# One branch of TensorE moved from behind the last layers to the middle of them, in a graph attention kernel

## The chip, the cores and the metric

The kernel runs on one core of a Trainium2 chip, in one launch. The metric is the device time in microseconds, median of three runs. A core has five engines with their own instruction streams: TensorE (matmuls), VectorE, ScalarE, POOL (GpSimd) and SyncE, which here issues the DMAs. They meet only at semaphores. Each engine has a sequencer that works through the stream (waits, branches, register reads) and hands the rest to the engine proper.

## The reference

Two blocks on 2048 nodes with 512 features: `x = x + smooth(relu(layernorm(x)), adj)` and `x = x + attend(relu(layernorm(x)), adj)`. The second one matters here:

```python
Wh = einsum('nf,hfd->hnd', x, W)                       # 8 heads of 64
e = leaky_relu(e_src[:, :, None] + e_dst[:, None, :], 0.2)
att = softmax(where(adj[None] > 0, e, -9e15), axis=-1)
h = elu(einsum('hnm,hmd->hnd', att, Wh))
enc = transpose(h, (1, 0, 2)).reshape(2048, 512)
out = relu(enc @ W1.T + b1)     # 512 -> 256
out = relu(out @ W2.T + b2)     # 256 -> 128
out = relu(out @ W3.T + b3)     # 128 -> 256
out = out @ W4.T + b4           # 256 -> 512
```

## The kernel before, in words

The attention is computed in factored form without a row maximum, which holds while the exponents and the row sums stay in a safe range. The kernel checks that range. A flag `retry` is 0 when all is in range; when it is 1, an exact attention (`attend_exactly`, a loop over tiles and heads) and the dense layers are computed again and the output is stored again. With the inputs given the flag is 0 and that path is jumped over.

After the attention the four dense layers run on four chunks of 512 nodes each, c = 0 to 3 (`CHUNKS` is 4). Class `Dense` holds the steps: `turn` transposes a quarter of the chunk's encoding, `sum1(c, m)` is one half of the first layer (12 matmuls), `sum2(c)` the second layer (6), `sum3(c)` the third (6), `sum_row(c, t)` the fourth layer for one tile of 128 nodes (6, and twice 6 half-wide ones for the last tile). Each product is split in high and low parts, hence three matmuls where one would stand. ScalarE applies the ReLUs (lines 2350 to 2367), VectorE cuts the low parts (2372 to 2382) and adds the residual rows (`finish_row`, 2290), POOL adds the bias to the residual (2297) and cuts two low parts (2301, 2304), SyncE stores the rows (2210), the last two chunks tile by tile, loads the residual (2202) and waits for the last stores (2222). The order on each engine is written out by hand; TensorE's stands in `dense_layers`, which takes the chunks interleaved: the next chunk's first layer between this chunk's second and third.

The flag is made like this. VectorE counts the row sums in range, per partition, into `fine_sum`; ahead of the third chunk's second layer (c = 2) TensorE adds the partitions up with a matmul of one column (line 1985); VectorE compares the count with what it should be and writes `retry` (line 1513). It raises `retry_chain`, on which the engines wait before they ask for the flag. To ask for it an engine reads the flag into a register and branches, in the helper `if_set`, line 86. VectorE does so at once, and has its remaining layer work in both arms of the branch. TensorE waits on `retry_chain` ahead of `sum3(2)`, since that writes the bank in which the count stood, but asks for the flag only behind all its layers, at line 2029. ScalarE, POOL and SyncE ask behind their last work too. The block's end (line 1327) is a drain on each engine and a meeting of all.

Of the kernel before, what the change touches and what calls it, by code (L numbers as in the profile page):

```python
# [81 lines left out]
def if_set(eng, flag):  # L82

    if flag is None:
        return nullcontext()
    return eng.If(eng.value_load(flag[0:1, 0:1], min_val=0, max_val=1) > 0)
# [1043 lines left out]
def attend_and_finish(nc, before, bank, wh, e, mask, ident, adj, e_rows, fac, wh_store, x1_store, weights, weight_parts, small, out):  # L1130
# [10 lines left out]
    with ExitStack() as ctx:  # L1141
# [3 lines left out]
        def sem(name):  # L1145
            return ctx.enter_context(nc.semaphore(name))
# [26 lines left out]
        retry, fine_sum, safe = small  # L1173
# [12 lines left out]
        with ExitStack() as later:  # L1186
            exact = attend_exactly(nc, ctx, later, bank, wh, e, ident, adj, e_rows, wh_store)
        exact_sync, exact_vector, exact_scalar, exact_tensor, exact_done = exact
        (parts_odd,), (_, e_late, _, *first_early), (res_odd, o3_hi, o3_lo, o2_hi, o2_lo, _) = one_place(
            nc, ctx, [("l4_parts1", [P, T, 2 * PW], F32R)],  # L1190
            [("l4_to_e_late", [P, 4224], F32), ("l4_e_late", [2 * H, 2 * QW], F32), ("l4_to_first", [P, 1024], F32), ("l4_first_a", [P, T - QUAD, HE], F32), ("l4_first_c", [P, T - QUAD, HE], F32)],
# [5 lines left out]
        src = sb("l4_src", [P, 2, QW])  # L1197
        o_m = sb("l4_o_m", [P, GT, PW])
        (whole,), (last_neg, _) = one_place(
            nc, ctx, [("l4_whole", [P, T, HE], F32)],  # L1200
            [("l5_last_neg", [P, 2, H, HD], F32), ("l5_rest_whole", [P, T], F32)])
# [54 lines left out]
        retry_chain = sem("l5_retry_chain")  # L1256
        fine_counted = sem("l5_fine_counted")
        dense_buffers = (share, neg, last_neg, (hi_even, hi_odd), (lo_even, lo_odd), (o1_hi, o1_lo), (o2_hi, o2_lo), (o3_hi, o3_lo), whole_o, (res_even, res_odd),
                         w1_hi, w1_lo, (w2_hi, w2_lo), (w3_hi, w3_lo), (w4_hi, w4_lo), b1_s, b2_s, b3_s, b4_s)
        dense = Dense(nc, ctx, "l5", EARLY, bank, wh, ident, dense_buffers)  # L1260
        again = Dense(nc, ctx, "l7", 0, bank, wh, ident, dense_buffers)
        CHUNKS = dense.NCH
# [64 lines left out]
        with nc.Block() as block:  # L1327
# [531 lines left out]
            def _(pe):  # L1859
# [109 lines left out]
                            pe.wait_ge(m_bank_free, GT * (LAST + 2))  # L1969
                        dense.turn(pe, 0, i // 2 - 2)  # L1970

                def dense_layers(of):
                    of.sum1(pe, 0, 0)
                    of.turn(pe, 1, 0)
                    of.turn(pe, 1, 1)
                    of.sum1(pe, 0, 1)
                    of.turn(pe, 1, 2)
                    of.turn(pe, 1, 3)
                    if of is dense:
                        pe.wait_ge(q_bank_free, GT * (2 * LAST + 3))  # L1980
                        pe.wait_ge(w_lo_ready, 4)
                    for c in range(CHUNKS - 1):
                        if of is dense and c == CHUNKS - 2:
                            pe.wait_ge(retry_chain, CHUNKS + 1)
                            pe.matmul(bank[of.SUM3_BANKS[0]][0:1, 0:1], fine_sum[:], safe[:], start=True, stop=True
                                      ).then_inc(fine_counted, 1)
                        of.sum2(pe, c)
                        of.sum1(pe, c + 1, 0)
                        if of is dense and c == CHUNKS - 2:
                            pe.wait_ge(retry_chain, CHUNKS + 2)  # L1990
                        of.sum3(pe, c)
                        of.sum1(pe, c + 1, 1)
                        of.sum_row(pe, c, 0)
                        if c + 2 < CHUNKS:
                            of.turn(pe, c + 2, 0)
                            of.turn(pe, c + 2, 1)
                        else:
                            of.sum2(pe, c + 1)
                        of.sum_row(pe, c, 1)
                        if c + 2 < CHUNKS:  # L2000
                            of.turn(pe, c + 2, 2)
                            of.turn(pe, c + 2, 3)
                        of.sum_row(pe, c, 2)
                        if c + 2 == CHUNKS:
                            of.sum3(pe, c + 1)
                        of.sum_row(pe, c, 3)
                    for t in range(GT):
                        of.sum_row(pe, CHUNKS - 1, t)

                pe.wait_ge(first_lo, 2)  # L2010
                for r in range(2):
# [12 lines left out]

                pe.wait_ge(w_loaded, 16 * 8)
                pe.wait_ge(w_lo_ready, 1)
                dense_layers(dense)
                pe.wait_ge(retry_chain, CHUNKS + 2)
                with if_set(pe, retry):
                    exact_tensor(pe)  # L2030
                    for k in range(KC):
                        again.turn(pe, 0, k)
                    dense_layers(again)


def attend_exactly(nc, ctx, tiles, bank, wh, e, ident, adj, e_rows, wh_store):
# [490 lines left out]
```

## Time and profile before

| | us |
|---|---|
| median of 3 runs | 861.61 (861.1 to 862.35) |
| the profiled execution | 862.1 |
| its span | 860.3 |
| TensorE busy | 839.7 |
| VectorE busy | 700.0 |
| ScalarE busy | 428.7 |
| POOL busy | 281.0 |

The profile is of one execution, whose own time is 862.1 us; the span, from the first to the last instruction of the program, is 1.8 us shorter. Times inside the trace count from the span's start. PE is TensorE's matmul, PEld its weight load, which overlaps the matmul before it; a q behind an engine's name is its sequencer. Register reads, branches, waits and DMA issues are not counted as busy; the view by source line shows them nevertheless. q1 are the data's DMA queues, q8 and q14 those by which instructions are fetched.

### The profile page before, as it was taken

Reading aid. Unit: us, or ns where it says so; the run is one execution under the profiler, and the core shown is the slowest. Engines: PE = TensorE matmul, PEld = TensorE weight load, DVE = VectorE, ACT = ScalarE, POOL = GpSimd, SP = SyncE. Lnnn points to the kernel's source line nnn. Section 1 sums busy time; section 2 is a strip of 40 time slices with the busy share of each in tenths; the row PEclk is TensorE's granted clock in tenths of the full one; section 3 lists DMA queues with packets and bytes.
Section 4 is the critical chain, followed back from the end, with each engine's and each line's share of the span. In section 5 each row is a group of like instructions: output and inputs, shape, how many; then the busy total and the mean of one; then the engine's idle time right before and its main releaser. Section 6 shows DMA issues by size and latency. Waiting matters only on the chain.

```text
span 860.3 us, 15286 instructions
## 1 busy us (share of the span) xinstructions
PE 839.7 (98%) x5208; PEld 756.5 (88%) x5208; DVE 700.0 (81%) x1222; ACT 428.7 (50%) x797; POOL 281.0 (33%) x299
## 2 busy tenths in 40 slices
PE   2999999999999999999999999999999999999997
PEld 2888888888888888888899999999999999999786
DVE  6899886557656886586999999999999999998864
ACT  3445433221111112257766666666666666775753
POOL 0000000000000000057875555555556654566422
PEclk9999999999999999999999999999999999999999
DMA  8979931703222222053310000000000032000134
GB/s 344 406 272 375 362 98 50 219 0 122 96 97 92 95 93 89 0 196 126 129 27 25 23 16 26 26 24 25 26 26 25 24 93 68 26 2 6 45 148 149
DMA packets 37675, 87.97 MB, mean 102 GB/s; under 512 B 7216, under 2 KB 8368, under 8 KB 37616
## 3 DMA queue, kind: packets, MB, share of 16 engines
q1 hardware_dynamic: 37616, 87.24, 28.5%
q8 instruction: 30, 0.49, 0.2%
q14 instruction: 29, 0.24, 0.1%
HBM read 74.45 MB, written 12.78 MB: 101 GB/s over the span
## 4 chain that ended last, share of the span: by engine, by line
PE 97%; DMA 1%; DVE 1%; ACT 1%; SPq 0%; issue 0%
PE bank L1877 29%; PE bank L1921 14%; PE bank L77 13%; PE bank L79 13%; PE bank L78 13%; PE bank L554 3%; PE bank L1082 2%; PE bank L1087 2%; PE bank L1083 2%; DMA l_kept<-adj 1%; PE bank L1033 1%; PE bank L2455 1%; PE bank L2449 1%; PE bank L2394 1%; PE bank L2451 1%; PE bank L2420 0%
## 5 line engine op out<-in xcount | busy, mean ns | idle before, releaser
L1397 DVE SCALAR_TENSOR_TENSOR l_q<-bank,e,mask 128x512 fp32r<-128x512 f32 x512 | 339.0, 740 | 22.9 <-PE bank L1877 22.9
L1877 PE MATMUL bank<-l_parts,l_q 128*128 128x260 f32 x2048 | 249.6, 283 | 0.0
L1877 PEld LDWEIGHTS bank<-l_parts,l_q 128*128 128x128 f32 x2048 | 246.7, 188 | 0.4
L77 PE MATMUL bank<-x_hi,s_hi 128*128 128x512 f32 x448 | 174.4, 389 | 0.0
L79 PE MATMUL bank<-x_hi,s_lo 128*128 128x512 f32 x448 | 174.3, 389 | 0.0
L78 PE MATMUL bank<-x_lo,s_hi 128*128 128x512 f32 x448 | 174.3, 389 | 0.0
L805 POOL TENSOR_TENSOR l_prod<-wh,l_a 128x512 f32<-128x512 f32 x29 | 34.0, 1195 | 379.5 <-ACT wh L757 379.5
L1565 ACT ACTIVATE l_o_q<-bank 128x260 f32<-128x260 f32 x128 | 49.0, 388 | 104.0 <-PE bank L1877 96.7
L79 PEld LDWEIGHTS bank<-x_hi,s_lo 128*128 128x128 f32 x448 | 84.1, 188 | 17.6
L78 PEld LDWEIGHTS bank<-x_lo,s_hi 128*128 128x128 f32 x448 | 84.1, 188 | 17.3
L77 PEld LDWEIGHTS bank<-x_hi,s_hi 128*128 128x128 f32 x448 | 84.1, 188 | 17.3
L734 ACT ACTIVATE s_hi<-rows 128x1024 fp32r<-128x1024 f32 x28 | 29.7, 1062 | 122.5 <-PE bank L79 122.5
L1559 ACT ACTIVATE l_mask_near<-mask 128x512 fp32r (+1 forms) x128 | 70.1, 621 | 1.3 <-DVE l_nmr L878 0.9
L1559 ACT ACTIVATE l_mask_far<-mask 128x512 fp32r (+1 forms) x128 | 69.9, 619 | 0.0
L1921 PE MATMUL bank<-l_parts,l_mask_far 128*128 128x260 f32 x512 | 67.7, 284 | 0.0
L1921 PE MATMUL bank<-l_parts,l_mask_near 128*128 128x260 f32 x512 | 67.3, 283 | 0.0
L1921 PEld LDWEIGHTS bank<-l_parts,l_mask_far 128*128 128x128 f32 x512 | 64.6, 189 | 0.0
L1921 PEld LDWEIGHTS bank<-l_parts,l_mask_near 128*128 128x128 f32 x512 | 64.3, 188 | 0.0
L824 DVE CAST x_hi<-G 128x512 fp32r<-128x512 f32 (+1 forms) x32 | 13.6, 426 | 50.8 <-PE bank L79 48.2
L1311 POOL TENSOR_TENSOR l_o_m<-l_o_m 128x520 f32<-128x520 f32 x16 | 18.5, 1157 | 82.3 <-ACT l_o_m L1572 82.3
L829 DVE TENSOR_TENSOR s_lo<-rows,s_hi 128x1024 fp32r<-128x1024 f32 x32 | 39.1, 1223 | 0.2 <-ACT s_hi L734 0.2
L463 ACT ACTIVATE s_hi<-l_now 128x1024 fp32r<-128x1024 f32 x16 | 17.0, 1060 | 39.1 <-PE bank L79 32.1
(234 smaller groups left out, 1179.8 us busy)
## 6 DMA issues: line engine op xcount, KB each, us to landing
rows<-adj_t SPq DMA_DIRECT2D x48, 512.0 KB, 3.8
l_now<-adj SPq DMA_DIRECT2D x16, 512.0 KB, 7.5
l_rows_k<-adj_t SPq DMA_DIRECT2D x16, 512.0 KB, 8.3
l_src<-e_rows SPq DMA_DIRECT2D x32, 256.0 KB, 3.2
l_kept<-adj SPq DMA_DIRECT2D x12, 512.0 KB, 13.2
wh_store<-wh SPq DMA_DIRECT2D x4, 1040.0 KB, 6.2
l_h<-x SPq DMA_DIRECT2D x4, 1024.0 KB, 17.3
x<-x SPq DMA_DIRECT2D x1, 4096.0 KB, 13.7
```

Of the source, the lines that this page charges most:

```text
L77: pe.matmul(acc, hi, rhs_hi, start=first, stop=False, skip_group_check=True)
L78: pe.matmul(acc, hi, rhs_lo, start=False, stop=False, skip_group_check=True)
L79: return pe.matmul(acc, lo, rhs_hi, start=False, stop=True, skip_group_check=True)
L554: mm = pe.matmul(bank[k][:], left[:, b, k * P:(k + 1) * P], right[:, s, :], start=s == 0 and n == 0, stop=n == 2, skip_group_check=True)
L734: a.activation(a_hi[:, r % 2, :], rows[:, r, :], ACT.Copy).then_inc(hi_ready, 1)
L805: p.tensor_tensor(per_head(prod[:, b, n, :]), wh[:, t, :, 0:HD], per_head(a_b[:, n, :]), ALU.mult).then_inc(prod_ready, 1)
L829: v.tensor_tensor(a_lo[:, b, :], rows[:, r, :], a_hi[:, b, :].bitcast(F32), ALU.subtract).then_inc(lo_ready, 1)
L1397: v.scalar_tensor_tensor(out=q[:, i, :], in0=bank[S_BANKS[hh]][:], scalar=e[:, i, H + h:H + h + 1], in1=mask[:, i, cols], op0=ALU.is_le, o ...
L1559: a.activation(mask_slot(i), mask[:, i, cols], ACT.Copy).then_inc(m_ready, 1)
L1565: a.activation(o_q[hh][:, t, :], bank[Q_BANKS[hh][t]][:, 0:PW], ACT.Copy).then_inc(q_bank_free, 1)
L1877: return pe.matmul(bank[Q_BANKS[hh][t]][:, 0:PW], q[:, i, t * P:(t + 1) * P], parts[pair_slot][:, i, hh * PW:(hh + 1) * PW], start=i == 0, ...
L1921: return pe.matmul(bank[M_BANKS[t]][:, 0:PW], mask_slot(i)[:, t * P:(t + 1) * P], parts[pair_slot][:, i, BOTH_C], start=i == 0, stop=i == ...
```

## The change

`dense_layers` is cut in two. `layers_up_to_count` holds everything up to the third chunk's second layer and the first half of the fourth chunk's first layer, with the matmul that counts ahead of them; `layers_from_count` holds the rest, from the third chunk's third layer on. TensorE now waits on `retry_chain` and asks for the flag between the two. The second part stands in both arms: with the flag set the exact path follows it, with the flag clear it is the `Else` arm. The order of the matmuls is the same as before in either case, and no other engine's program is changed.

```diff
-                def dense_layers(of):
+                def layers_up_to_count(of):
...
-                    for c in range(CHUNKS - 1):
-                        if of is dense and c == CHUNKS - 2:
-                            pe.wait_ge(retry_chain, CHUNKS + 1)
-                            pe.matmul(bank[of.SUM3_BANKS[0]][0:1, 0:1], fine_sum[:], safe[:], start=True, stop=True
-                                      ).then_inc(fine_counted, 1)
+                    for c in range(CHUNKS - 2):
                         of.sum2(pe, c)
                         of.sum1(pe, c + 1, 0)
-                        if of is dense and c == CHUNKS - 2:
-                            pe.wait_ge(retry_chain, CHUNKS + 2)
                         of.sum3(pe, c)
...
+                    if of is dense:
+                        pe.wait_ge(retry_chain, CHUNKS + 1)
+                        pe.matmul(bank[of.SUM3_BANKS[0]][0:1, 0:1], fine_sum[:], safe[:], start=True, stop=True
+                                  ).then_inc(fine_counted, 1)
+                    of.sum2(pe, CHUNKS - 2)
+                    of.sum1(pe, CHUNKS - 1, 0)
+
+                def layers_from_count(of):
+                    c = CHUNKS - 2
+                    of.sum3(pe, c)
+                    of.sum1(pe, c + 1, 1)
+                    of.sum_row(pe, c, 0)
+                    of.sum2(pe, c + 1)
+                    of.sum_row(pe, c, 1)
+                    of.sum_row(pe, c, 2)
+                    of.sum3(pe, c + 1)
+                    of.sum_row(pe, c, 3)
                     for t in range(GT):
-                        of.sum_row(pe, CHUNKS - 1, t)
+                        of.sum_row(pe, c + 1, t)
...
-                dense_layers(dense)
+                layers_up_to_count(dense)
                 pe.wait_ge(retry_chain, CHUNKS + 2)
                 with if_set(pe, retry):
+                    layers_from_count(dense)
                     exact_tensor(pe)
                     for k in range(KC):
                         again.turn(pe, 0, k)
-                    dense_layers(again)
+                    layers_up_to_count(again)
+                    layers_from_count(again)
+                with pe.Else():
+                    layers_from_count(dense)
```

## Rows read from the trace of the kernel before

**Rows 1.** The page: busy time, share, instructions; the chain's shares by engine.
```profile
PE 839.7 (98%) x5208; PEld 756.5 (88%) x5208; DVE 700.0 (81%) x1222; ACT 428.7 (50%) x797; POOL 281.0 (33%) x299
...
PE 97%; DMA 1%; DVE 1%; ACT 1%; SPq 0%; issue 0%
```
**Rows 2.** Line 86: operation, count: ns min/median/max, first and last start in us.
```profile
L86 DVEq TENSOR_LOAD <-retry x1: 550/550/550, 834.0 to 834.0; - x1
...
L86 DVEq COMPARE_BRANCH  x1: 56/56/56, 834.9 to 834.9; - x1
...
L86 PEldq TENSOR_LOAD <-retry x1: 482/482/482, 854.1 to 854.1; - x1
...
L86 PEldq COMPARE_BRANCH  x1: 4147/4147/4147, 855.0 to 855.0; - x1
```
**Rows 3.** Line 1327, the end of the block.
```profile
L1327 PEldq DRAIN  x1: 72/72/72, 859.2 to 859.2; - x1
...
L1327 SPq DRAIN  x1: 7/7/7, 860.1 to 860.1; - x1
```
**Rows 4.** DMA queues in the window 856.0 to 856.1: packets, MB, share of 16 engines.
```profile
q8 instruction: 1, 0.02, 107.6%
```
**Rows 5.** Timeline 832.5 to 833.9: start us, length us, engine, line, operation, tiles.
```profile
833.80 0.14 DVE L1513 TENSOR_SCALAR retry<-bank 1x1 int32<-1x1 f32 x1
```
**Rows 6.** Line 2236 in the window 832 to 834, TensorE's sequencer.
```profile
L2236 PEldq EVENT_SEMAPHORE  x1: 2393/2393/2393, 833.2 to 833.2; - x1
```
**Rows 7.** Timeline: the third layer's first weight load; the last two matmuls.
```profile
837.14 0.19 PEld L2431 LDWEIGHTS bank<-l_o_hi,l_w_hi 128*128 128x128 f32 x1
...
855.35 0.40 PE L2455 MATMUL bank<-l_w_hi,l_o_lo 128*128 128x256 f32 x2
```
**Rows 8.** Timeline of SyncE at 833.91; DMA queues in 835.0 to 837.8.
```profile
833.91 0.38 SPq L2210 DMA_DIRECT2D out<-l_res  x1
...
q1 hardware_dynamic: 496, 0.99, 94.6%
```
**Rows 9.** DMA queues in 837.8 to 838.2; timeline of VectorE with its idle time.
```profile
q14 instruction: 1, 0.01, 4.8%
...
839.99 0.69 DVE L2382 TENSOR_TENSOR l_o_lo<-bank,l_o_hi 128x512 fp32r<-128x512 f32 x1 [6.05 <-ACT bank L2367]
```
**Rows 10.** DMA queues in 830 to 831.
```profile
q8 instruction: 1, 0.02, 8.2%
```
**Rows 11.** Timeline of POOL, VectorE and TensorE's weight loads in 844 to 851.
```profile
844.02 4.63 POOL L2297 TENSOR_TENSOR l_res<-l_res,l_b 128x2048 f32<-128x2048 f32 x1 [3.82 <-DMA l_res<-x_store]
...
850.81 1.44 DVE L2290 TENSOR_TENSOR l_res<-bank,l_res 128x512 f32<-128x512 f32 x2
...
850.95 0.19 PEld L2455 LDWEIGHTS bank<-l_w_hi,l_o_lo 128*128 128x128 f32 x1 [0.43 <-DVE l_o_lo L2382]
```
**Rows 12.** Line 2210: all stores; landing of that in 846 to 847; in 856 to 857.
```profile
L2210 SPq DMA_DIRECT2D out<-l_res x11: 332/333/1869, 818.2 to 856.2; - x11
...
DMA to landing us min/median/max: 2.0/2.0/2.0
...
DMA to landing us min/median/max: 3.6/3.6/3.6
```
**Rows 13.** DMA packets in 857.2 to 857.75; line 2222, the wait for the last store.
```profile
DMA packets 1, 0.00 MB, mean 4 GB/s; under 512 B 0, under 2 KB 0, under 8 KB 1
...
L2222 SPq EVENT_SEMAPHORE  x1: 17/17/17, 859.9 to 859.9; - x1
```
**Rows 14.** Engines' busy time by window (matmuls of one tile), then all; PEclk after PE.
```profile
16.00:18.00 2.00, 2.00 (x5) 1.61 (x6) 0.00 (x0) 0.00 (x0) 1.00 1.03 410
18.00:20.00 2.00, 2.00 (x6) 1.52 (x6) 0.00 (x0) 0.00 (x0) 1.00 1.03 410
...
22.00:24.00 2.00, 2.00 (x11) 1.65 (x10) 0.00 (x0) 0.00 (x0) 1.00 1.03 410
...
856.00:860.30 4.30, 0.00 (x0) 0.00 (x0) 0.21 (x1) 0.00 (x0) 0.00 (x0) 1.00 0.36 118
```

More of the change, by code:

```diff
@@ L1993, in dense_layers @@
                         of.sum_row(pe, c, 0)
[L1994 to L1998, printed above, removed]
+                        of.turn(pe, c + 2, 0)
+                        of.turn(pe, c + 2, 1)
                         of.sum_row(pe, c, 1)
-                        if c + 2 < CHUNKS:
-                            of.turn(pe, c + 2, 2)
-                            of.turn(pe, c + 2, 3)
+                        of.turn(pe, c + 2, 2)
+                        of.turn(pe, c + 2, 3)
                         of.sum_row(pe, c, 2)
-                        if c + 2 == CHUNKS:
-                            of.sum3(pe, c + 1)
                         of.sum_row(pe, c, 3)
+                    if of is dense:
[14 more added lines that the diff above has]
+                    of.sum_row(pe, c, 3)
                     for t in range(GT):
-                        of.sum_row(pe, CHUNKS - 1, t)
+                        of.sum_row(pe, c + 1, t)
                 pe.wait_ge(first_lo, 2)
```

## The prediction, made before the result was known

> **What bounds the kernel now.** I read the page first: its busy times and the chain that ended last [rows 1]. TensorE is busy for 98% of the span and holds 97% of the chain, so nearly every microsecond in which TensorE stands in the last layers reaches the end. The timeline of 820 to 861 us says the same of the place of the change: weight load follows weight load every 0.23 us, and the flag is made beside it.
>
> The second view is by source line, since a branch is not counted as busy. Line 86 reads the flag into a register and branches [rows 2]. On VectorE the pair begins at 834.0 and the branch itself is booked with 56 ns. On TensorE it stands at the end of everything: the read begins at 854.1, the branch at 855.0, and the branch is booked with 4147 ns. TensorE's drain follows at 859.2 while SyncE's own drain is at 860.1 [rows 3]. So TensorE's closing branch does not end the kernel itself. It is what the change moves into the middle of the layers.
>
> The third view is the DMA activity in short windows, because such a branch has a visible cause: an instruction fetch. A 16 KB packet on the instruction queue q8 starts in the window 856.0 to 856.1; it takes 107.6% of 16 engines over 0.1 us, which is 1.72 us on one [rows 4]. It starts 1.0 us after the branch, and the branch ends (855.0 + 4.15 = 859.15) 3.1 us after the fetch began.
>
> **The change part by part.**
>
> *Order of the matmuls.* They are the same ones in the same order on the path taken here (flag clear). Two conditionals on the chunk number disappear at build time. Cost 0, with nothing that could hide one: no queue but TensorE's is touched. DMAs, SyncE and POOL keep their programs.
>
> *What stands between flag and branch.* The flag is ready at 833.80 + 0.14 = 833.94 [rows 5], and VectorE's read starts at 834.0. TensorE's sequencer can be there in time, because it runs ahead of its array: an event of the third chunk's third layer (line 2236), which stands behind all of the third chunk's second layer and the first half of the fourth's first, is already under way at 833.2 [rows 6], while the first matmul of that third layer loads its weights only at 837.14 [rows 7]. The end of the kernel agrees: the read at 854.1 comes while the last two matmuls run from 855.35 on. So I start TensorE's new read at 834.0 and its branch 0.9 us later (854.1 to 855.0), at 834.9. Until 837.14 the array has work queued. That is a cover of 2.2 us from the branch on.
>
> *The branch.* With the 4.15 us of rows 2 it would end at 839.05, the next weight load would come about 0.1 later, and TensorE would stand for 839.1 - 837.1 = 2.0 us. But there is a difference in what the DMA engines do. The new branch falls into the 1 MB store issued at 833.91: from 835.0 to 837.8 data packets hold 94.6% of the 16 engines and no code packet is seen [rows 8]. VectorE's branch of 834.9 jumps over a large body as well, and the first code packet of any engine after it starts between 837.8 and 838.2, behind the store [rows 9], 3 us after the branch and not 1.0. VectorE never shows this, since it waited for ScalarE's second relu half until 839.99 anyway [rows 9]. I take that packet to be VectorE's, and let TensorE's fetch wait as long. From its start the branch takes 3.1 us by rows 4, less what a quieter queue saves: a 16 KB fetch in the window 830 to 831 took 8.2% of 16 engines, 1.3 us instead of 1.72 [rows 10]. So 837.8 + 2.8 = 840.6, and TensorE stands for 840.6 - 837.2 = 3.4 us. Bounds: 0 if the branch were as short as VectorE's 56 ns (833.94 + 0.9 + 0.1 = 834.9, all covered); 2.0 with a prompt fetch; 3.9 with 3.1 us from the fetch's start; 5.3 if the array had to be empty before the read (837.5 + 0.9 + 4.15 = 842.5 against 837.2). I take 3.4, nearest to rows 8 and 9.
>
> *Behind the branch.* Queued behind it are TensorE's last 84 matmuls; ScalarE waits for the third layer, VectorE for rest and rows, SyncE for the rows to store. Nothing absorbs: TensorE's waits after 838, such as the 0.43 us at 850.95 [rows 11], are for results of matmuls that themselves move. The bias addition of the last chunk on POOL (844.02, 4.63 long) is due at 850.81 [rows 11], so a residual load delayed by the fetch has 2.2 us of air, and 3.4 more after the shift. The stall goes to the end in full.
>
> *What leaves the end.* The last stores do not land like the others. A store issued in 846 to 847 lands in 2.0 us; the last one, issued at 856.24, takes 3.6, and its issue takes 1869 ns where the median is 333 [rows 12]. This is the time of the 16 KB fetch of TensorE's closing branch. Between 857.2 and 857.75 just one data packet is seen in 0.55 us, when 128 KB or more should be moving [rows 13]: one engine holds back its part and the issue stands behind it. SyncE finds the last landing at 859.9 [rows 13], 0.4 before the end. With the closing branch gone, the store should land in 2.0 to 2.2 us: 3.6 - 2.05 = 1.55 us saved. SyncE's own read and branch, 0.9 us as on the other engines, move up with the issue: 856.6 + 0.9 = 857.5, before the landing at 858.3. Bounds 0 (SyncE's issue was slow for a reason of its own) and 1.6.
>
> *Sum.* 862.1 (the profiled execution: span 860.3 and 1.8 around it) + 3.4 - 1.55 = 863.95. The median of the runs, 861.61, lies 0.5 below the profiled one, which gives 863.45; I say 863.4, 0.21% slower.
>
> The Trainium skill, page "Runtime: NRT & Kernel Launch", section "Instruction fetch mechanics", says a taken branch whose target is outside the current 2-page window forces a DMA fetch, and gives TensorE 128 KiB for instructions. The trace agrees with the fetch (4147 ns). If it were the 128 KiB that counted, the target could be at hand, which is rival B.
>
> **The rivals.**
>
> *A, the fetch is prompt.* It goes ahead of the store's packets as at 856.0, where stores were moving too. The stall is 2.0: 862.1 + 2.0 - 1.55 = 862.55, by the median 862.05, no change. For it: the only measured TensorE case. Against it: the empty code queues of rows 8. It decides at the fetch's start: before 837 it is A, behind it the forecast.
>
> *B, the branch finds its target.* All is covered by the queued matmuls and only the end changes: 861.6 - 1.55 = 860.05, faster by 0.18%, and just over 0.2% if the end gives back 0.2 more. Against it: the same kind of jump missed at 855.0, and the new one spans more. This is the mechanism on the other side; it holds as long as the branch is under 2.2 us.
>
> *C, the end gives nothing back.* The slow issue was SyncE's own, or a prefetch of TensorE's next page falls into the last 2 us: 861.6 + 3.4 = 865.0, or 863.6 with A's stall. For it: SyncE's code may miss as well; against: the single trickling packets just while q8 was fetching.
>
> *D, a second stop.* If the branch's target lies near the end of its page, TensorE runs dry again while the next page comes, by an estimate from the fetch above (1.3 us, and the 1.4 from the fetch's end at 857.7 to the branch's at 859.15) 2 to 3 us: 865.4 to 866.4. At 0.23 us for a weight load with its matmul, that is the last two dozen instructions of a page.
>
> *E, the clock.* TensorE starts at half its later rate, though the clock's column prints 1.00 there: 5 matmuls from 16 to 18 us and 6 from 18 to 20, 11 from 22 to 24 [rows 14]. If it fell from 2.4 to 1.2 GHz after the stop and stayed there for those 4 us, that costs 2 more, 865.4. Against it: after the last matmul the granted clock stays 1.00 over 4.3 idle us [rows 14].
>
> The Trainium skill, "TensorE: Matmul & The Clock Gate", section "Why this matters for your kernels", warns that idle gaps between matmul bursts put the clock back; by it E would be the outcome. The trace shows no stop of that length in mid-kernel, and none at its end that cost clock.
>
> **How the numbers follow.** Forecast 0.40, A 0.27, B 0.08, C 0.10, D 0.10, E 0.05. A measurement of this kernel tells about 0.2% (1.7 us) from no change, so 863.35 is the line. The forecast (862.9 to 864.1 by its bounds) lies on both sides of it: 0.23 slower, 0.17 same. A is same. B gives 0.06 faster, 0.02 same. C splits 0.08 to 0.02; D and E are slower by 0.13, and 0.02 of D is same with A's stall. Together 0.06 faster, 0.50 same, 0.44 slower. The range goes from B's edge to D: 860.6 to 865.6.
>
> **What would show it.** In the changed trace, line 86 on TensorE: its read at 834.0 and a branch of 5.5 to 6.1 us (A: 4.1; B: under 0.3). The q8 packet behind 837.6 (A: before 836.5). An idle time before line 2431's weight load of 3.4 us (A: 2.0). The last store's issue at 0.33 us and its landing at 2.0 to 2.2 us. TensorE's count and order of matmuls unchanged. The forecast fails if TensorE does not stand at the branch, or if the last store still takes 3.6 us to land.

## The result and the profile after

The changed kernel takes 866.56 us (median; 865.96 to 866.91), the kernel before 861.63: a ratio of 1.0056, with a 95% interval of 1.0043 to 1.0069. It is slower by 4.9 us. The forecast was 863.4 with a range to 865.6, so the time lies outside it. The profiled execution took 866.76 us, with a span of 864.8 against 860.3.

The page after: TensorE's busy time grew from 839.7 to 842.7 us with the same number of matmuls [rows 1], which no stop alone can do. VectorE's did not move.

```profile
PE 842.7 (97%) x5208; PEld 758.7 (88%) x5208; DVE 700.0 (81%) x1222; ACT 429.2 (50%) x797; POOL 281.4 (33%) x299
...
PE 97%; DVE 1%; DMA 1%; ACT 1%; issue 1%
```

By line, line 86 after (answers to rows 2) and the drains of line 1327 (rows 3):

```profile
L86 DVEq TENSOR_LOAD <-retry x1: 552/552/552, 833.6 to 833.6; - x1
L86 PEldq TENSOR_LOAD <-retry x1: 478/478/478, 833.6 to 833.6; - x1
...
L86 PEldq COMPARE_BRANCH  x1: 5710/5710/5710, 834.5 to 834.5; - x1
...
L1327 PEldq DRAIN  x1: 1682/1682/1682, 860.0 to 860.0; - x1
```

TensorE reads the flag in the same tenth of a microsecond as VectorE, with matmuls still queued on the array until 837.1, and the branch takes 5.71 us where the closing one took 4.15. Everything up to there lies 0.38 us earlier than in the trace of before. The timeline of TensorE around the stop (start, length, engine, line; in brackets the idle time before):

```profile
836.76 0.39 PE L79 MATMUL bank<-l_enc_t_hi,l_w_lo 128*128 128x512 f32 x1
...
840.30 0.29 PEld L2440 LDWEIGHTS bank<-l_o_hi,l_w_hi 128*128 128x128 f32 x1 [3.58 <-issue]
840.33 0.77 PE L2440 MATMUL bank<-l_o_hi,l_w_hi 128*128 128x512 f32 x1 [3.18 <-issue]
...
840.89 0.63 PE L2441 MATMUL bank<-l_o_hi,l_w_lo 128*128 128x512 f32 x1
...
841.32 0.63 PE L2443 MATMUL bank<-l_o_lo,l_w_hi 128*128 128x512 f32 x1
```

The third layer's first weight load (line 2440, before 2431, rows 7) is at 840.30; without a stop it would be at 837.14 - 0.38 = 836.76. So the stop is 3.5 us. And then the matmuls do not come every 0.23 us but every 0.43. The windows show why (busy time of PE, PEld, DVE, ACT, POOL; then the granted clock, DMA share, GB/s):

```profile
830.00:837.00 7.00, 7.00 (x32) 5.26 (x31) 2.72 (x5) 1.88 (x4) 3.46 (x2) 1.00 0.39 141
837.00:840.30 3.30, 0.14 (x1) 0.00 (x1) 0.00 (x0) 1.27 (x2) 1.34 (x2) 0.90 0.38 60
...
839.50:840.00 0.50, 0.00 (x0) 0.00 (x0) 0.00 (x0) 0.00 (x0) 0.29 (x1) 0.62 0.98 57
...
840.30:846.40 6.10, 6.07 (x14) 4.79 (x15) 1.38 (x2) 2.48 (x4) 2.20 (x1) 0.50 0.42 162
...
850.00:855.00 5.00, 5.00 (x24) 4.14 (x23) 2.14 (x5) 2.53 (x5) 0.00 (x0) 1.00 0.34 132
```

The granted clock was 1.00 (2.4 GHz) until the stop and fell within it: the mean of 0.62 in 839.5 to 840.0 puts the fall at 839.6, 2.5 us after the last matmul's end (836.76 + 0.39 = 837.15). It stood at 0.50 (1.2 GHz) until 846.4, for 6.8 us in all, and in the last 6.1 of them TensorE was working. In these 6.1 us 14 to 15 matmuls ran; at full rate they need 3.4 us.

The q8 packet and the last stores (rows 8, 9, 12 and 13 of before). First the DMA queues: the q1 line is of the window 834.5 to 837.4, which has no q8 or q14 packet, and the q8 and q14 lines are of 837.4 to 838.4. Then line 2219, the stores, with the landing of the last:

```profile
q1 hardware_dynamic: 515, 1.03, 96.0%
...
q8 instruction: 1, 0.02, 5.9%
q14 instruction: 1, 0.01, 1.9%
```
```profile
L2219 SPq DMA_DIRECT2D out<-l_res x11: 332/333/388, 817.9 to 862.2; - x11
...
DMA to landing us min/median/max: 2.2/2.2/2.2
```

No code packet starts while the 1 MB store runs; then one on each code queue does. No store is slow to issue any more, and the last lands in 2.2 us, not 3.6.

No second stop follows: the next q8 packet starts at 843.4, and the weight loads around it keep their distance of 0.43 us.

The balance of the two traces: -0.38 (earlier arrival) + 3.54 (the stop) + 2.76 (the half clock: from the third layer's first weight load to that of the first row it is 847.14 - 840.30 = 6.84 us, before 841.22 - 837.14 = 4.08) - 1.4 (the end: VectorE's last addition at 861.71 against 855.78, 5.93 later, the span's end only 4.5 later) = 4.5 us, the difference of the spans.

### The profile page after: what moved, and what is told of

It reads as the page before. It is cut to its first block, busy times and chain, and to the rows that moved or that the text cites. A ratio compares the mean times of both kernels' runs of the same rounds, so it can differ in the third digit from the quotient of the medians.

```text
span 864.8 us, 15286 instructions
## 1 busy us (share of the span) xinstructions
PE 842.7 (97%) x5208; PEld 758.7 (88%) x5208; DVE 700.0 (81%) x1222; ACT 429.2 (50%) x797; POOL 281.4 (33%) x299
## 4 chain that ended last, share of the span: by engine, by line
PE 97%; DVE 1%; DMA 1%; ACT 1%; issue 1%
PE bank L1877 28%; PE bank L1921 14%; PE bank L79 13%; PE bank L78 13%; PE bank L77 13%; PE bank L554 3%; PE bank L1082 2%; PE bank L1087 2%; PE bank L1083 2%; PE bank L1033 1%; PE bank L2464 1%; PE bank L2458 1%; PE bank L2403 1%; PE bank L2460 1%; DMA l_h<-x 1%
```

## The experiments

Each is compared with the kernel before as timed beside it: its median was 861.39 us for near, no_branch, warm14 and tiles_after, 861.54 for idle, tiles_before and hint, and 861.62 for the other three.

**near: a short jump.** TensorE's arm for a set flag, not taken here, is cut to the layers.

```diff
                     layers_from_count(dense)
-                    exact_tensor(pe)
-                    for k in range(KC):
-                        again.turn(pe, 0, k)
-                    layers_up_to_count(again)
-                    layers_from_count(again)
                 with pe.Else():
```

> The changed kernel, but TensorE's arm for a set flag holds only the layers; the exact path and the repeated layers are left out on TensorE alone (that arm is not taken here). The jump to the clear arm is then short. Theory (the instruction fetch makes the branch long, the stop puts the clock back, and a closing fetch disturbs the last store): TensorE's branch under 0.3 us, no idle time ahead of the third chunk's third layer, granted clock 1.000, last store lands in 2.0 to 2.3 us; 861.6 - 1.45 = 860.2. Rival (a register read and a branch between queued matmuls cost by themselves, wherever the target lies): branch over 4 us or a stop of over 2 us, 864 or more.

860.03 against 861.39 us, ratio 0.9983 (0.9974 to 0.9992), granted clock 1.000. Line 86 and the stores:

```profile
L86 PEldq COMPARE_BRANCH  x1: 461/461/461, 834.7 to 834.7; - x1
```
```profile
L2214 SPq DMA_DIRECT2D out<-l_res x11: 332/332/388, 818.1 to 856.1; - x11
...
DMA to landing us min/median/max: 1.7/1.7/1.7
```

The branch takes 0.46 us (I expected under 0.3), TensorE does not stand at it, and the last store lands in 1.7 us. So a branch at this place costs nothing that shows when its target is near; with the far target it costs the stop and what follows from it.

**no_branch: the end by itself.** The kernel before without TensorE's closing question.

```diff
                 dense_layers(dense)
-                pe.wait_ge(retry_chain, CHUNKS + 2)
-                with if_set(pe, retry):
-                    exact_tensor(pe)
...
-                    dense_layers(again)
```

> The kernel before without TensorE's closing question for the flag (its exact path is left out on TensorE). Theory (the code fetch of TensorE's closing branch holds back one DMA engine, and with it the last store): the last store is issued in 0.33 us and lands in 2.0 to 2.3 us, 861.6 - 1.45 = 860.2. Rival (SyncE's slow issue is its own, and the changed kernel's last store was quicker because it came later): last issue 1.9 us, landing 3.6, 861.6.

860.27, ratio 0.9990 (0.9981 to 0.9999): faster by 0.9 us by the ratio and by 1.1 by the medians, where 1.45 was expected; the interval, 0.1 to 1.6 us, leaves room for both. The longest issue and the last landing:

```profile
L2204 SPq DMA_DIRECT2D out<-l_res x11: 332/332/389, 817.3 to 855.4; - x11
...
DMA to landing us min/median/max: 1.7/1.7/1.7
```

Nothing of SyncE or the stores was touched, and the slow issue (1869 ns) and the slow landing (3.6 us) of rows 12 are gone. So TensorE's closing branch did reach the end of the kernel, through the DMA engine that carried its code.

**warm14: the stop filled.** 14 matmuls whose result is not used are queued ahead of the read.

```diff
                 layers_up_to_count(dense)
+                dense.wait_for_rest(pe, 3, CHUNKS - 3, 1)
+                for n in range(14):
+                    pe.matmul(bank[dense.SUM3_BANKS[1]][:], dense.w1_hi[:, 0, 0:P], dense.enc_t_hi[1][:, 0, :],
+                              start=True, stop=True, skip_group_check=True)
                 pe.wait_ge(retry_chain, CHUNKS + 2)
```

> The changed kernel with 14 matmuls of 512 columns, whose result is not used, queued on TensorE just ahead of the flag's read; they write a bank that the third layer then overwrites. They fill 3.2 us of the 3.5 us stop. Theory (the clock falls because the array stands): branch 5.7 us as before it, third layer begins at 840.3, granted clock 1.000, 866.5 - 2.7 = 863.8; if the queue cannot take them all, the read comes late and it is up to 864.8. Rival (the clock falls for another reason than the idle time, as the fetch or the branch itself): clock 0.996 and 866.5 or more.

864.13, ratio 1.0032 (1.0020 to 1.0044), clock 1.000. With 3.2 us of work more it is 2.4 us faster than the changed kernel. Line 86, then the timeline:

```profile
L86 PEldq TENSOR_LOAD <-retry x1: 864/864/864, 836.7 to 836.7; - x1
...
L86 PEldq COMPARE_BRANCH  x1: 3400/3400/3400, 837.9 to 837.9; - x1
```
```profile
837.56 3.33 PE L2035 MATMUL bank<-l_enc_t_hi,l_w_hi 128*128 128x512 f32 x14
841.48 0.47 PE L2444 MATMUL bank<-l_o_hi,l_w_hi 128*128 128x512 f32 x1 [0.59 <-issue]
841.78 0.40 PE L2445 MATMUL bank<-l_o_hi,l_w_lo 128*128 128x512 f32 x1
```

The flag's read came at 836.7, 2.5 us after VectorE's at 834.2, I take it because the queue could not hold all 14, and the layer begins at 841.5 and not 840.3. What remains is a stop of 0.6 us between matmuls, and behind it they come at full rate. The branch, later than the 1 MB store, takes 3.4 us. It is still a far branch with a code fetch, and the clock holds.

**tiles_after and tiles_before: the store out of the fetch's way.** The second chunk's rows go out in four stores of 256 KB as they are finished.

```diff
-        step = 1 if c >= self.NCH - 2 else self.GT
+        step = 1 if c >= self.NCH - 3 else self.GT
```

with the counts of two waits on the stores' semaphore to match.

> The changed kernel, in which the second chunk's rows are stored tile by tile as they are finished (four stores of 256 KB) and not in one of 1 MB that is issued just before the branch. Theory (the code fetch waits behind the 1 MB store): the fetch starts about 1 us after the branch, the branch takes 4.2 us or little more, TensorE stands 2.0 us; if the clock then holds, 862.3, if it falls all the same 865.0. Rival (the branch takes 5.7 us because of its farther target or the fetch itself): branch 5.7 us, 866.5.

> The kernel before with the second chunk's rows stored tile by tile, the control for the changed kernel with that edit. Theory (that edit matters only where a fetch waits behind the 1 MB store): 861.4, within 0.5. Rival (the four small stores are quicker by themselves and hid a stop): 860 or less.

In the changed kernel: 861.92, ratio 1.0005 (0.9996 to 1.0014), clock 1.000. In the kernel before: 861.91 against 861.54, ratio 1.0004 (0.9995 to 1.0013), no change. Line 86 and the code packets in 835.6 to 836.0, first edit:

```profile
L86 PEldq COMPARE_BRANCH  x1: 3634/3634/3634, 834.6 to 834.6; - x1
```
```profile
q8 instruction: 1, 0.02, 16.6%
q14 instruction: 1, 0.01, 5.9%
```

The third layer's first weight load, and a window behind it:

```profile
838.35 0.19 PEld L2440 LDWEIGHTS bank<-l_o_hi,l_w_hi 128*128 128x128 f32 x1 [1.50 <-issue]
...
838.40:846.00 7.60, 7.60 (x34) 6.30 (x35) 2.67 (x4) 4.34 (x8) 5.93 (x2) 1.00 0.29 109
```

The two code packets start 1.2 us after the branches and not 3.3, TensorE's branch takes 3.6 us and not 5.7, its weight loads stand for 1.5 us (the idle time of line 2440), and the clock holds. The same jump with the same matmuls, and 4.4 to 4.6 us less than the changed kernel (4.4 when each is taken against the kernel before beside it): by the traces 2.0 of the stop and 2.8 of the clock. The control says that the edit has no gain of its own.

**idle: a stop without a branch.** The kernel before with one wait more, ahead of the third chunk's third layer.

```diff
                             pe.wait_ge(retry_chain, CHUNKS + 2)
+                            pe.wait_ge(of.pool_done, of.NCH + 1)
                         of.sum3(pe, c)
```

> The kernel before with one wait more and no branch moved: ahead of the third chunk's third layer TensorE waits for POOL's rest of the fourth chunk's first layer, which ends at 840.2. TensorE then stands about as long as in the changed kernel (weight load at 840.3 and not 837.1), without branch or code fetch there. Theory (any stop of this length puts the clock back): granted clock under 1.000, matmuls every 0.43 us for some us after the stop, 861.4 + 3.1 + 2.7 = 867.2, the last store still landing in 3.6 us. Rival (the clock falls only with the branch or the fetch): clock 1.000, 861.4 + 3.1 = 864.5.

866.35, ratio 1.0046 (1.0033 to 1.0060). The weight loads, and a window behind the stop:

```profile
840.27 0.19 PEld L2432 LDWEIGHTS bank<-l_o_hi,l_w_hi 128*128 128x128 f32 x1 [3.13 <-issue]
...
841.14 0.33 PEld L2432 LDWEIGHTS bank<-l_o_hi,l_w_hi 128*128 128x128 f32 x1
841.57 0.33 PEld L2433 LDWEIGHTS bank<-l_o_hi,l_w_lo 128*128 128x128 f32 x1
```
```profile
840.60:843.80 3.20, 3.20 (x9) 2.43 (x9) 0.69 (x1) 1.95 (x4) 0.00 (x0) 0.50 0.81 314
```

A plain wait puts the clock down as well, here for half as long: finer windows put the fall at 840.5 and the rise at 843.9. That is 3.1 us of stop and some 1.7 of clock (half of 3.4 us), 866.3 with 861.54, and not the 867.2 expected from a clock term of 2.7. And it does not do so every time. Of the five executions four ran at a mean granted clock of 0.998 and took 865.57 to 866.58 us; the fifth kept 1.000 and took 864.35, close to the rival's 864.5. So a stop like this seems able to pass without the loss; that execution has no trace of its own. The closing branch is still there, and so are the last store's slow issue of 1634 ns and slow landing of 3.4 us.

**hint, hint_late, hint_before, hint_before_early: the branch announced.** An instruction ahead of the branch names it as likely taken. In hint it runs at 821.8, 13 us ahead of the branch; in hint_late at 830.6, 4.6 us ahead; in hint_before at 833.1 and in hint_before_early at 817.5, 21 and 38 us ahead of the closing branch. The edit of hint, in the complete changed kernel:

```diff
+                        if of is dense and c == 1:
+                            far_arm.append(pe.mark_branch_hint_location())
                         of.sum1(pe, c + 1, 1)
...
+                asked_in = pe.bass.cur_bb.bb
                 with if_set(pe, retry):
...
+                bass.BassInstruction(asked_in.instructions[-1]).branch_hint(far_arm[0])
```

> The changed kernel, complete, with a branch prefetch hint on TensorE: at the second chunk's third layer, some 10 us ahead of the branch, the branch is announced as likely taken. Theory (only the late fetch of the clear arm costs): if the hint fetches the clear arm in advance, branch under 0.5 us, no stop, clock 1.000, last store landing in 2.0 to 2.3 us, 860.1, faster than both kernels. If the hint fetches the arm that is not taken here, or is dropped at the page crossed at 830, everything is as in the changed kernel, 866.5, or worse by a wrong fetch. Rival (the stop is not the fetch): 866 with the code packet seen early.

860.18 against 861.54, ratio 0.9983 (0.9974 to 0.9992): faster than both kernels, with both arms complete. Line 86 and the weight loads at the branch's place:

```profile
L86 PEldq COMPARE_BRANCH  x1: 506/506/506, 834.9 to 834.9; - x1
```
```profile
836.94 0.19 PEld L79 LDWEIGHTS bank<-l_enc_t_hi,l_w_lo 128*128 128x128 f32 x1
837.17 0.19 PEld L2446 LDWEIGHTS bank<-l_o_hi,l_w_hi 128*128 128x128 f32 x1
```

A q8 packet starts at 830.9, where the changed kernel has one too (830.5), and the next only at 838.2, well behind the branch. That this packet now carried the clear arm is the likely reading; no view shows what a packet holds.

> The changed kernel with the hint just ahead of the matmul that counts, after the page crossed at 831 or close to it. Theory 1 (fetch at once): the packet starts near 832 to 833 and ahead of the 1 MB store, the branch ends by 836, under the 2.2 us that queued matmuls cover: 860.2. Theory 2 (only a page's crossing fetches): the branch takes 5.7 us, TensorE stands 3.5 us, the clock falls, 866.5.

> The kernel before, complete, TensorE's closing branch left where it is and announced by a prefetch hint ahead of the third chunk's third layer, some 20 us earlier. Theory 1 (the hint makes the sequencer fetch the target at once): code packet near 833, closing branch under 0.6 us, last store landing in 2.0 to 2.3 us, 860.2. Theory 2 (the hint only turns the next fetch at a page's crossing to the target; in the kernel with the early hint the instruction ran at 821.8 and the packet came at 830.9): no page is crossed between 831 and 855, the branch stays at 4 us, 861.5.

> The same, announced at the second chunk's third layer, ahead of the page crossed at 831. Both theories: one code packet at 831 or before, closing branch under 0.6 us, last store landing in 2.0 to 2.3 us, 860.2. It tells whether the branch had to be moved at all for the gain of the moved and announced one (860.2): if so this stays at 861.5.

The late hint does nothing for the branch, which takes 5.7 us, and the stop is 3.6: 865.27, ratio 1.0036 (1.0024 to 1.0048). Nor do the two in the kernel before: 861.39 and 861.37, both 0.9993 (0.9984 to 1.0002), closing branches of 4147 and 3987 ns. For the late one and for hint_before it is as theory 2 had it: the hint ran 0.6 us ahead of the q8 packet at 831.2, or behind the one at 830.0, and no other code packet came before the branch. The early hint in the kernel before I expected to work, by both theories, and it did not. So the rule by which a hint is kept or dropped is open. Of four places one gave a gain, 13 us ahead of the moved branch; that the branch must be moved for a gain is not shown.

hint_late is also the changed kernel's stop once more, and yet it is 1.3 us faster than the changed kernel. The wait at the third layer (line, releaser, total, times, longest), and two windows:

```profile
PEld bank L2445 <- issue: 3.6, 1, 3.6
...
841.00:844.30 3.30, 3.23 (x8) 2.59 (x9) 0.30 (x1) 1.52 (x3) 0.00 (x0) 0.50 0.79 302
844.30:846.00 1.70, 1.70 (x9) 1.40 (x8) 1.09 (x2) 0.95 (x2) 1.43 (x1) 0.98 0.00 0
```

The clock fell here too, at 841.0, but for 3.4 us and not 6.8. So the length of the stop alone does not set what the clock costs.

## Why the prediction was wrong

*The order of the matmuls, the read.* Right. TensorE's read stands beside VectorE's at 833.6, and near shows that read and branch hide behind queued matmuls.

*The branch.* Right in mechanism and size. Forecast: a fetch that waits for the 1 MB store, a branch of 5.5 to 6.1 us, a stop of 3.4. Measured: 5.71 and 3.5. That the stop fits this well is in part luck: the branch ended 2.4 us after the q8 packet's start and not 2.8, and the layers were 0.4 us early, which made the stop that much longer. tiles_after moves the store away and the packet comes 2.2 us sooner, the branch is 2.1 us shorter. Rival A (a prompt fetch, stop of 2.0) is what that kernel shows (1.5), and its time, 862.05, is close to the 861.92 measured. It fell for the changed kernel. Rival B (the target at hand, a branch under 0.3 us) fell with the branch of 5.71.

*D, a second stop.* There was none.

*Nothing absorbs.* Right: VectorE's last addition is later by the whole of stop and clock.

*What leaves the end.* Right in mechanism: forecast 1.55, measured 1.4 in the two traces and 0.9 to 1.1 in no_branch, so rival C (nothing given back) fell. The last store landed in 2.2 us, and in 1.7 in near and no_branch. The changed kernel still fetches a page near the end, at 860.1, and those two fetch none while the last stores run; that this makes the difference is not shown.

*The sum.* 3.4 - 1.55 is 1.85, and the measured difference 4.9. The step that failed is rival E, the clock, held at 0.05: "Against it: after the last matmul the granted clock stays 1.00 over 4.3 idle us". The row is right and the conclusion was not. It shows one stop in which the clock held, and I read it as saying that a shorter one cannot put it down. In the changed kernel the fall came 2.5 us after the last matmul's end, within the 3.2 us between two matmuls, and the half clock that followed cost 2.76 us. The term was also too small: 2 us from the 4 us at the kernel's start, against these 2.76, since TensorE worked at half clock for over 6 us. With E as the likeliest case my own terms give 863.4 + 2 = 865.4, and with the measured size 866.2. The Trainium skill's page "TensorE: Matmul & The Clock Gate", section "Why this matters for your kernels", warns of idle gaps between matmul bursts, and it was the better guide. The changed kernel's four executions agree with it at a stop of 3.5 us, and so do four of idle's five at 3.1; the fifth does not.

*Shown and not shown.* Shown by runs: that the far target makes the branch long (near, hint), that the store delays its fetch (tiles_after), that a stop without a branch puts the clock down in most executions, and a far branch with only a short stop does not (idle, warm14, tiles_after), that the closing fetch held up the last store (no_branch). Not shown: that VectorE's q14 packet is what rows 9 took it for, though it moved with TensorE's in tiles_after; why one execution of idle kept its clock; and why the half clock lasted 6.8 us in the changed kernel and 3.4 in idle and hint_late.

## What to carry to other kernels

A branch over a large body takes TensorE's sequencer 3.4 to 4.15 us here, and 5.7 beside a large store, of which the queued matmuls hide about 2; with a near target it takes 0.46. Ask by line what each sequencer's branch takes, since the busy table does not show it. When a change makes TensorE stand, price the clock behind the stop as well as the stop, and take a row in which it held as one draw and not as a bound. Code comes over the same DMA engines as data, so a fetch is slow beside a large store (its packet starts 3.3 us after the branch and not 1.2), and a small last store is slow beside a fetch (it lands in 3.6 us and not 1.7 to 2.2).

## What the runs showed of the hardware that was not expected

- With a stop of 3.1 to 3.6 us in mid-kernel the granted clock went to 0.50 for 6.8 us (the changed kernel) or 3.4 (idle, hint_late), and in one of idle's five executions it did not fall; with stops of 1.5 us (tiles_after) and 0.6 us (warm14) it stayed 1.00.
- One 16 KB code fetch turned a 0.33 us store issue into 1.87 and a landing of 1.7 to 2.2 us into 3.6.
- A branch hint took a far branch on TensorE from 5.7 to 0.5 us in one place and did nothing in three others.
